# One tile of layer 0's squared pair sums becomes a plain product on VectorE

## The reference

```python
xk = x0
for W in (W0, W1, W2):            # (32, 32, 64), (32, 64, 64), (32, 64, 64)
    xk = relu(einsum('bmd,bhd,mhk->bkd', x0, xk, W))
    outs.append(sum(xk, axis=2))
h = concatenate(outs + [dense_ctx], axis=1)     # 192 + 16 columns
y = relu(relu(h @ W_top1 + b_top1) @ W_top2 + b_top2) @ W_top3
```

## Time and profile before

| | |
|---|---|
| median of three runs | 651.62 us (650.42 to 654.16) |
| profiled execution | 651.33 us, span 649.5 us |
| TensorE busy | 593.5 us (91%) |
| VectorE busy | 542.6 us (84%) |
| GpSimd busy | 441.0 us (68%) |
| ScalarE busy | 399.5 us (62%) |
| moved by DMA | 104.57 MB, 161 GB/s on average |

### The profile page before, as it was taken

One profiled execution on the slowest core, in us unless ns is written; L12 is line 12 of the kernel. 1 busy time (PEld: TensorE's weight loads), 2 busy tenths in 40 slices (PEclk: granted clock), 3 DMA queues, 4 the chain that ended last, 5 costly groups with the idle time before them and its releaser, 6 DMA issues.

```text
span 649.5 us, 7363 instructions
## 1 busy us (share of the span) xinstructions
PE 593.5 (91%) x2580; PEld 187.3 (29%) x2580; DVE 542.6 (84%) x292; ACT 399.5 (62%) x644; POOL 441.0 (68%) x303
## 2 busy tenths in 40 slices
PE   0158699799999999999999999999999999999897
PEld 0012122233332333333333333333333333322243
DVE  0039889799899998989898989898999989899700
ACT  0041554967676777858586767676767778666032
POOL 5737766678897788889898988885989842522000
PEclk9998799999999999999999999999999999999999
DMA  3296989897978786959596968687877869030000
GB/s 102 70 248 145 225 190 235 205 221 194 216 197 193 207 181 182 207 157 214 144 213 169 196 168 200 150 213 149 211 167 197 179 188 194 32 64 0 9 9 0
DMA packets 41671, 104.57 MB, mean 161 GB/s; under 512 B 16897, under 2 KB 25665, under 8 KB 33442
## 3 DMA queue, kind: packets, MB, share of 16 engines
q1 hardware_dynamic: 32562, 100.53, 64.5%
q0 software_dynamic: 8192, 2.11, 3.6%
q10 hardware_dynamic: 880, 1.46, 0.8%
HBM read 99.08 MB, written 4.20 MB: 159 GB/s over the span
## 4 chain that ended last, share of the span: by engine, by line
PE 77%; DMA 7%; DVE 5%; issue 4%; POOL 4%; SPq 2%; ACT 1%; DVEq 0%
PE acc L531 59%; PE pair_sum L503 4%; DVE prod L330 4%; POOL gath L256 4%; PE pair_sum L518 4%; PE pair_sum L511 3%; DMA x_scratch<-gath 3%; PE pair_sum L524 2%; PE rep L589 2%; DMA gath<-in_tables,rows_sb 2%; DMA x_rot<-x_scratch 1%; SPq L231 1%; PE rep L581 1%; PE rep L582 1%; DVE z_sb L335 0%
## 5 line engine op out<-in xcount | busy, mean ns | idle before, releaser
L330 DVE TENSOR_TENSOR prod<-m_rep,rep 128x2048 f32<-128x2048 f32 x227 | 503.1, 2281 | 15.5 <-PE acc L531 11.2
L531 PE MATMUL acc<-prod,w_sb 128*64 128x512 f32 x1816 | 410.5, 601 | 18.4 <-DVE prod L330 16.5
L418 ACT COPY rep<-state 32x512 f32<-32x512 f32 x504 | 292.6, 581 | 52.2 <-DVE prod L330 45.3
L256 POOL DMA_INDIRECT gath<-in_tables,rows_sb x256 | 244.2, 954 | 94.8 <-issue 77.5
L531 PEld LDWEIGHTS acc<-prod,w_sb 128*64 128x64 f32 x1816 | 126.1, 138 | 295.9 <-issue 254.8
L267 POOL TENSOR_TENSOR prod_pool<-m_rep,xb 128x2048 f32<-128x2048 f32 x29 | 132.6, 4571 | 50.2 <-ACT xb L428 34.3
L267 POOL TENSOR_TENSOR prod_pool<-x_rot,x_rep 128x2048 f32<-128x2048 f32 x14 | 64.0, 4572 | 12.0 <-DMA x_rot<-x_scratch 9.0
L503 PE MATMUL pair_sum<-x0c,sel_sb 32*128 32x512 f32 x128 | 38.0, 670 | 26.7 <-DMA x0c<-x_scratch 25.5
L390 ACT ACTIVATE state<-pair_sum 128x512 f32<-128x512 f32 x16 | 9.6, 597 | 79.9 <-PE pair_sum L524 79.9
L531 PE MATMUL acc<-prod_pool,w_sb 128*64 128x512 f32 x232 | 54.7, 592 | 0.0
L411 ACT ACTIVATE sums_sq<-pair_sum 128x1024 f32<-128x1024 f32 x32 | 32.9, 1027 | 33.5 <-PE pair_sum L503 33.5
(11 more groups left out here) (27 smaller groups left out, 84.4 us busy)
## 6 DMA issues: line engine op xcount, KB each, us to landing
m_rep<-x_scratch SPq DMA_DIRECT2D x256, 256.0 KB, 9.4
x_rot<-x_scratch SPq DMA_DIRECT2D x32, 512.0 KB, 5.8
x_rep<-x_scratch SPq DMA_DIRECT2D x16, 512.0 KB, 3.8
gath<-in_tables,rows_sb POOLq DMA_INDIRECT x256
x_scratch<-gath SPq DMA_DIRECT2D x16, 256.0 KB
x0c<-x_scratch SPq DMA_DIRECT2D x32, 64.0 KB
w_sb<-in_w ACTq DMA_DIRECT2D x2, 512.0 KB, 4.6
m_rep<-z_sb SPq DMA_DIRECT2D x12, 64.0 KB, 2.3
```

Of the source, the lines that this page charges most:

```text
L256: pool.indirect_dma_start(out=gath[p % 2][:, g, :], out_offset=None, in_=tables, in_offset=bass.IndirectOffsetOnAxis(ap=rows_sb[:, n:n + 1 ...
L330: nc.vector.tensor_tensor(prod[:, number % RING], in0, in1[:, None, :].to_broadcast([128, 2, PAIR]), ALU.mult).then_inc(unit_ready, 1)
L418: last = nc.scalar.copy(rep[v][M * q:M * q + M, CHUNK * a:CHUNK * a + CHUNK], state[l - 1][K * a + M * v:K * a + M * v + M, :])
L531: last = nc.tensor.matmul(acc[K * a:K * a + K, :], w, src[:, k, CHUNK * a:CHUNK * a + CHUNK], start=start and k == 0, stop=stop and k == 1)
```

## The change

Of the four tiles of pairs, three are now products and one is squared pair sums. The third product has its own source, x_rot2, loaded by SP (512 KB more for each pair, and one more wait ahead of the loads of x: own_ready), and its own result, x_own. It is made by VectorE (`own_layer0`, 128x1024, both inputs in SBUF): for p = 0 and 1 right behind `first_layer0`, for p = 2 behind unit 1 of slot 2, for p = 3 to 15 behind unit 4 of slot (1, p-1). All who wait for the rows of x now wait for four loads, not three. TensorE makes one pair sum for each pair, behind unit 0 (the one behind unit 3, or behind unit 1 of slots 1 and 2, is gone), and in layer 0 the two matmuls of the second sums_sq tile become two of x_own, behind the products. ScalarE makes one square. The scratch for loading the weights of layer 0 (wa_sb, wb_sb, wd_sb, selt_sb) lies in the last buffer of the ring, and the biases and last weights of the dense layers lie in a spare tile of m_rep.

```diff
-XT = 2
-QB = 2
+XT = 3
+PT = 2
+QB = 1
-SUMS_AT = (0, 3)
+SUMS_AT = (0,)
...
-        x_rot = sb("x_rot", [128, XT, PAIR])
+        x_rot = sb("x_rot", [128, PT, PAIR])
+        x_rot2 = sb("x_rot2", [128, PAIR])
+        x_own = sb("x_own", [128, PAIR])
...
+        wa_sb = prod[:, RING - 1, 0, 0:ST * K].rearrange("r (t k) -> r t k", k=K)
+        wb_sb = prod[:, RING - 1, 0, ST * K:2 * ST * K].rearrange("r (t k) -> r t k", k=K)
+        wd_sb = prod[0:2 * M, RING - 1, 1, 0:K]
+        selt_sb = prod[:, RING - 1, 1, K:K + QB * 2 * M].rearrange("r (t m) -> r t m", m=2 * M)
...
+        b1_sb = m_rep[:, spare + 4, 0:F1 // 128]
+        b2_sb = m_rep[:, spare + 4, 8:8 + F2 // 128]
+        wt3_sb = m_rep[:, spare + 4, 16:16 + F2 // 128]
...
                 if p > 0:
                     x_multiplied(sp, p - 1)
+                    sp.wait_ge(own_ready, p)
...
                 for t in range(XT):
...
-                    sp.dma_start(x_rot[:, t, :], src).then_inc(x_in, 16)
+                    dst = x_rot[:, t, :] if t < PT else x_rot2[:, :]
+                    sp.dma_start(dst, src).then_inc(x_in, 16)
...
             def first_layer0(p):
...
+                own_layer0(p)
+
+            def own_layer0(p):
+                dve.wait_ge(x_in, 16 * (1 + XT) * (p + 1))
+                after(dve, l0_done, p)
+                nc.vector.tensor_tensor(x_own[:, :], x_rot2[:, :], x_rep[:, :], ALU.mult).then_inc(own_ready, 1)
...
                     if (i, n) == (1, 1):
                         first_layer0(1)
+                    if (i, n) == (2, 1):
+                        own_layer0(2)
+                    if i >= 3 and l == 1 and p + 1 < NP and n == 4:
+                        own_layer0(p + 1)
...
             square(0, 0)
-            square(0, 1)
...
-                if i >= 3 and nxt is not None:
-                    square(nxt, 1)
...
+                pe.wait_ge(own_ready, p + 1)
+                for a in range(2):
+                    nc.tensor.matmul(acc0[K * a:K * a + K, :], w0_sb[:, PT, :], x_own[:, CHUNK * a:CHUNK * a + CHUNK],
+                                     start=False, stop=False)
...
-            pair_sums(0, 1)
...
-                    if i in (1, 2) and n == 1:
-                        pair_sums(i, 1)
```

More of the change, by code:

```diff
@@ L98, in build @@
         m_rep = sb("m_rep", [128, M_BUFS * T, PAIR])
-        wa_sb = sb("wa_sb", [128, ST, K])
-        wb_sb = sb("wb_sb", [128, ST, K])
         w0_sb = sb("w0_sb", [128, ST, K])
-        wd_sb = sb("wd_sb", [2 * M, K])
         wdiag_sb = sb("wdiag_sb", [2 * M, K])
         sel_sb = sb("sel_sb", [2 * M, QB, 128])
-        selt_sb = sb("selt_sb", [128, QB, 2 * M])
         w_sb = [None, sb("w1_sb", [128, 2, T, K]), sb("w2_sb", [128, 2, T, K])]
-        b1_sb = sb("b1_sb", [128, F1 // 128])
-        b2_sb = sb("b2_sb", [128, F2 // 128])
-        wt3_sb = sb("wt3_sb", [128, F2 // 128])
         state = [sb(f"state{l}", [128, CHUNK]) for l in range(3)]
@@ L155, in build @@
         first_x = sem("first_x")
+        own_ready = sem("own_ready")
         first_rep = sem("first_rep")
@@ L324, in first_layer0 @@
                 dve.wait_ge(x_in, 16 * (1 + XT) * (p + 1))
-                nc.vector.tensor_tensor(prod_pool[:, p], x_rot[:, :, :], x_rep[:, None, :].to_broadcast([128, XT, PAIR]),
+                nc.vector.tensor_tensor(prod_pool[:, p], x_rot[:, :, :], x_rep[:, None, :].to_broadcast([128, PT, PAIR]),
                                         ALU.mult).then_inc(first_x, 1)
+                own_layer0(p)
[3 more added lines that the diff above has]
+                nc.vector.tensor_tensor(x_own[:, :], x_rot2[:, :], x_rep[:, :], ALU.mult).then_inc(own_ready, 1)
             def unit(number, in0, in1):
@@ L451, in _ @@
                     square(i, 0)
-                    square(i, 1)
                     relu0(i)
@@ L515, in layer0 @@
                 at = p if p < 2 else POOL_AT[("x", p)] % POOL_RING
-                for t in range(XT):
+                for t in range(PT):
                     for a in range(2):
```

## The result

The changed kernel takes 674.13 us (median of six runs, 670.38 to 682.14) against 652.89 for the kernel before in the same sessions. The ratio is 1.032, with a 95% interval of 1.030 to 1.035: about 21 us slower. The slowest of the six, 682.14 us, counts as a slow run and is not in the ratio. The forecast was 14 us slower, with a range up to 22: the direction is right, the size short by a third, and the result lies just inside the end of the range. The profiled execution took 677.24 us with a span of 675.4, which is 25.9 over the profiled execution of before; all that follows is measured in it.

The account below looks back on a forecast made before the run. TensorE was taken to set the pace, VectorE 1.74 us behind. 651.33 us plus 12.4 (start) plus 1.6 (steady state) gave 665.3, as a median 665.6 us; range 656 to 674.

Parts of the forecast that it names:

- What bounds the kernel, what TensorE saves: Steady state: TensorE sets the 34.47 us period; one pair of sums less saves it about 1.2 us, alone 33.3 us.
- The loop of the steady state: VectorE's product ahead of units 5 and 6 closes a loop of 34.60 us against 34.47: +1.6 us over 12 periods.
- the loop theory: Product ahead of units 5 and 6 loses TensorE's 1.2 us; behind the slot's last unit, period 33.8 us, about 652.
- the line between reduction and product: VectorE's 1024-element product, interpolated between 512-element reduction and 2048-element product: 1.13 us in a run, 1.21 alone.
- The start: Before the steady state: extra load costs 2.1 us a pair, adding up over p = 0 to 3; 12.4 us later.
- (A): VectorE's two-SBUF product and GpSimd's product of x exclude each other: 670 us, 674 with one later crossing; chance 0.25.
- (B): Start: extra loads slip into DMA gaps, +4.7 us at p = 2, +5.7 at p = 3, 659 us; chance 0.20.
- (C): Steady state: product vanishes in VectorE's 1.74 us idle time, TensorE keeps 1.2 us a period; 649.6 or 643 us; chance 0.10.

Follow-up runs that it names:

- the kernel that reads PSUM: The changed kernel, but from p = 1 on the new product takes its second factor from the replicated state in PSUM, not x_rep: 663.56 us, ratio 1.017.

## Why the prediction was right in direction and short in size

**What bounds the kernel, what TensorE saves.** Right. The period was TensorE's, and the pair of sums taken away gave nothing while the product stood ahead of units 5 and 6.

**The loop of the steady state.** Right: 34.60 us forecast, 34.51 measured, TensorE's idle time 0.81 instead of some 1.1 us. Moving the product out of the loop gave 33.68, which the loop theory had at 33.8. The product took 1.22 us alone, 1.13 in a run (181.38 to 182.51), as the line between reduction and product had said.

**The start.** Right in sum, by luck: its parts were wrong and made up for each other. Without collisions it was 11.95 us instead of 12.4. But the load did not add up to 2.1 us a pair. In the four profiled runs that load x_rot2 on the chips without late loads, the first x product started at 39.08 to 41.21 us, with 38.70 before, and the rows of p = 2 landed at 104.9 to 107.0 and not at 108.5. VectorE stood 2.93 us for them in the kernel that reads PSUM, and not at all in the changed kernel, instead of 6 to 7. In place of the rest stood TensorE's slow pace, which the forecast did not have. Layer 0 of p = 0 ended at 48.12 us in the kernel that reads PSUM, 4.1 later than before, with the rows only 0.4 later. About 1 us of this is no matter of pace: the matmuls on x_own wait for the rows, while the matmuls on sums_sq that they replace ran ahead of them, and the forecast had this exchange at 0. And at p = 2, behind a wait of 5.60 us, that kernel's two units took 5.65 us instead of some 3.7.

**The step that failed** is the choice between forecast and (A). Both kernels had the same evidence, a gather stretched to 2.04 us; I gave (A) 0.25, since VectorE might be first. It came true for p = 2 and 3 in both profiled runs of kernels that left both engines free to start, and once or twice more later. By its own sum (A) was 670 us, and 674 with one later crossing, and two terms of that sum were too small.

The first is p = 3. (A) had VectorE there just as GpSimd ends, at no cost; VectorE came 2.05 us behind GpSimd's start and lost 2.4 us. The second is what comes behind a collision: TensorE stands still, its clock falls, and its next units run at half of it. (A) had that at nothing. Step by step against the kernel that reads PSUM, the first two collisions are 2.3 us at the product of p = 2 (4.2 for the collision, less the 1.9 by which it started earlier), 0.5 behind it, 2.4 at the product of p = 3 and 1.2 behind it: 6.45, where (A) had 4.4. The later crossing is 4.4 and 2.4 behind it: 6.86, where (A) had up to 4.5. Summed up, 651.8 + 11.95 + 6.45 + 0.5 = 670.7 with no later crossing, and one more makes 677.5: the lowest run was 670.38, the profiled one 677.24. That the spread of the runs is the number of late crossings is argued from two runs, not shown, since only one of them has a trace.

**(B)**, the cheap start, was half true: loads landed earlier than forecast, but TensorE's slow pace took it back, and nothing was won. **(C)** fell: it needed the product outside the loop, and there it held to 0.8 of the 1.2 us.

**The Trainium skill**, "SBUF — State Buffer", section "Who interferes with whom": its rule now agrees in both directions. GpSimd first: VectorE ends 1.09 us behind it, three times in three; VectorE first: gathers of 1.78 us instead of 0.95. And with one input in PSUM there is no contention, as the same section states: both products at 107 us kept their usual 1.22 and 4.51 us.

## What to carry to other kernels

An engine's idle time can be used only by work that stands where the idle time is: the same 1.13 us of work cost all of TensorE's saving ahead of two units and only a third of it behind them. Before giving VectorE an operation with two inputs in SBUF, look at what GpSimd does at that moment; if both can come to their instructions at the same time, write down their order, for one wait was worth some 9 us here. And price a new wait of TensorE with what comes behind it, the stretch at half clock.

## What was not expected of the hardware

- A collision stretches VectorE's instruction in the profile (3.6 to 5.6 us for 1.22) and is not shown as idle time. The mean of the group (1914 ns) was the first sign; without it the product looks merely slow.
- TensorE's granted clock was at 0.50 behind waits of 4.97 us (after the third collision) and 5.60 us (p = 2, the kernel that reads PSUM). In the usual period, with waits of 0.26 and 0.55 us, it stayed at 1.00.
- The kernel before took 651.8 us on one chip and 673 to 675 us on two others. Where kernels differ by 1%, only runs of one session can be compared.
